# Two dispatch scatters in flight at most, in a two-layer MoE kernel on one core

## What is computed

```python
    x = x + _L0_ffn_ref(_L0_cond_ref(x, itok_B_0_15, L0_cond_weights, L0_cond_b), ...)
    x = x + _L1_ffn_ref(_L1_cond_ref(x, itok_B_0_8, L1_cond_W1, ...), ...)
```

## Time and profile before

| | us |
|---|---|
| median of 3 timed runs | 514.65 (514.14 to 516.04) |
| span of the profiled execution | 571.1 |
| PE busy in it | 463.1 (81%) |
| DVE / ACT / POOL busy | 261.9 / 255.9 / 238.0 |
| on the chain that ended last: PE | 63% |
| on the chain that ended last: another core or an unknown queue | 10% |

### The profile page before, as it was taken

The page is one execution under the profiler, slowest core; times in us unless marked ns, Lnnn a source line. Parts: engine busy times, 40 slices in busy tenths (PEclk is TensorE's granted clock), DMA queues, the critical chain, the costliest instruction groups (busy, mean ns, idle before and its releaser), DMA issues.

```text
span 571.1 us, 10130 instructions
## 1 busy us (share of the span) xinstructions
PE 463.1 (81%) x3132; PEld 392.7 (69%) x3133; DVE 261.9 (46%) x831; ACT 255.9 (45%) x596; POOL 238.0 (42%) x255
## 2 busy tenths in 40 slices
PE   6897698978888889999846765489999999999910
PEld 3785564566676766787744655178999999999900
DVE  1144267845555554347447912053433333233475
ACT  2453453235555543556314241034455555555653
POOL 2023535214554555003272777600155555556550
PEclk8997879999999999999787796579999999999975
DMA  9999921102222107400010111110223434313569
GB/s 242 365 340 368 367 66 37 39 23 67 74 71 63 47 11 235 143 2 20 19 51 15 48 48 55 42 47 1 61 76 96 134 107 113 105 50 88 165 182 282
DMA packets 70930, 62.33 MB, mean 109 GB/s; under 512 B 9676, under 2 KB 57439, under 8 KB 70898
## 3 DMA queue, kind: packets, MB, share of 16 engines
q1 hardware_dynamic: 63202, 48.32, 28.5%
q0 software_dynamic: 7168, 12.56, 6.7%
q10 hardware_dynamic: 528, 1.05, 0.6%
HBM read 32.44 MB, written 31.69 MB: 112 GB/s over the span
## 4 chain that ended last, share of the span: by engine, by line
PE 63%; another core or an unknown queue 10%; DVE 9%; DMA 7%; issue 6%; ACT 2%; POOL 1%; SPq 0%; DVEq 0%; POOLq 0%; ACTq 0%
PE PS L1645 11%; PE PS L1304 8%; PE PS L1361 6%; PE PS L1603 5%; PE PS L1441 3%; PE PS L1635 3%; PE PS L1565 3%; PE PS L1633 3%; PE PS L1634 3%; PE PS L1393 2%; PE PS L1402 2%; DMA back1b<-grp_y,grp_i 2%; PE PS L1426 2%; PE PS L1428 1%
## 5 line engine op out<-in xcount | busy, mean ns | idle before, releaser
L623 POOL DMA_INDIRECT back<-grp_y,grp_i x70 | 69.8, 997 | 93.9 <-DVE grp_y L1236 71.0
L605 POOL DMA_INDIRECT rows<-disp,slot x64 | 63.6, 994 | 76.1 <-DVE slot L1072 56.0
L1645 PE MATMUL PS<-w2r,act 128*128 128x128 f32 x640 | 78.1, 275 | 0.5 <-ACT act L789 0.5
L1645 PEld LDWEIGHTS PS<-w2r,act 128*128 128x128 f32 x640 | 74.8, 192 | 0.9 <-DVE grp_y L1236 0.7
L582 POOL DMA_INDIRECT back<-act,blk_i x48 | 46.9, 977 | 60.8 <-DVE act L1015 41.1
L789 ACT ACTIVATE act<-PS,b1r 128x256 f32<-128x256 f32 x160 | 63.7, 477 | 16.5 <-PE PS L1635 14.2
L571 POOL DMA_INDIRECT rows<-disp,slot x32 | 32.6, 1018 | 67.4 <-issue 53.8
L1236 DVE TENSOR_TENSOR grp_y<-PS,b2r 128x256 f32<-128x256 f32 x40 | 17.0, 424 | 89.6 <-PE PS L1645 69.5
L1603 PE MATMUL PS<-sw,act 128*128 128x128 f32 x256 | 37.5, 313 | 14.1 <-issue 11.8
L1633 PE MATMUL PS<-xh,w1h 128*128 128x256 f32 x160 | 48.3, 302 | 0.0
L740 ACT ACTIVATE act<-PS,sb 128x512 f32<-128x512 f32 x32 | 21.4, 688 | 59.6 <-remote 32.9
(11 more groups left out here) (256 smaller groups left out, 1009.9 us busy)
## 6 DMA issues: line engine op xcount, KB each, us to landing
rows<-zrow SPq DMA_DIRECT2D x32, 260.0 KB, 5.0
grp_x<-rows SPq DMA_DIRECT2D x40, 130.0 KB
w_raw<-in_f_gate_up SPq DMA_DIRECT2D x8, 512.0 KB, 10.1
back<-zrow SPq DMA_DIRECT2D x8, 512.0 KB
back<-back SPq DMA_DIRECT2D x16, 256.0 KB, 5.0
blk_x<-rows SPq DMA_DIRECT2D x48, 65.0 KB
acc<-in_x SPq DMA_DIRECT2D x8, 256.0 KB, 5.8
y0g<-back SPq DMA_DIRECT2D x8, 256.0 KB, 3.2
```

Of the source, the lines that this page charges most:

```text
L605: gp.indirect_dma_start(rows1, bass.IndirectOffsetOnAxis(ap=slot[:, k, t:t + 1], axis=0), disp[:, t, :], None, bounds_check=E1 * CAP - 1, ...
L623: gp.indirect_dma_start(back, bass.IndirectOffsetOnAxis(ap=grp_i[v % NX][:, u:u + 1], axis=0), grp_y[k][:, u, :], None, bounds_check=last, ...
L1645: last = mm(PS[5 + k][:, u * P:(u + 1) * P], act[k][:, c, u * P:(u + 1) * P], w2r[e][:, c, :], start=c == 0, stop=c == C1 - 1)
```

## The change

Each dispatch scatter but the first two of each layer waits until the scatter two before it has landed. For that the semaphores are shared out otherwise: by the parity of the tile, not by group (layer 0) or by half (layer 1). The wait for the whole half ahead of the rewrite of the codes goes away, since the new waits imply it.

```diff
+                if t >= 2:
+                    pool.wait_ge(sc0[t % 2], 16 * (t // 2))
                 gp.indirect_dma_start(rows0, bass.IndirectOffsetOnAxis(ap=slot[:, 0, t:t + 1], axis=0),
                                       disp[:, t, :], None, bounds_check=NBLKP * P - 1,
-                                      oob_is_err=False).then_inc(sc0[t // G % 2], 16)
+                                      oob_is_err=False).then_inc(sc0[t % 2], 16)
...
+                    n = k * NT + t
+                    if n >= 2:
+                        pool.wait_ge(sc1[(n - 2) // NT][t % 2], 16 * ((n - 2) % NT // 2 + 1))
                     gp.indirect_dma_start(rows1, bass.IndirectOffsetOnAxis(ap=slot[:, k, t:t + 1], axis=0),
                                           disp[:, t, :], None, bounds_check=E1 * CAP - 1,
-                                          oob_is_err=False).then_inc(sc1[k][t // HT], 16)
+                                          oob_is_err=False).then_inc(sc1[k][t % 2], 16)
                     if (k, t) in ((0, NT - 8), (1, HT - 8)):
                         h = k
-                        pool.wait_ge(sc1[0][h], 16 * HT)
```

## The result

The changed kernel takes 538.61 us (median of 4 runs, 538.06 to 540.67) and the kernel before 514.76 (4 runs beside it, 514.14 to 516.04): a ratio of 1.0458 with a 95% interval of 1.0412 to 1.0503, slower by 23.9 us. The forecast was 522.2 in a range of 513 to 529, so the sign was right, the size was a third of the real one, and the range did not hold it. The profiled execution took 538.72 us and has a span of 536.6. Its own time fits the span and the median; the span of the first profile (571.1) did not.

What follows compares the result with a forecast made beforehand. Without stalls, layer 1's dispatch scatters were taken to bound the expert phase. Layer 1 adds 9 us, 1.5 lost to slack, layer 0 adds 0: 514.65 + 7.5 = 522.2 us, range 513 to 529.

Steps and rivals of the forecast that it cites:

- The stalls are of one execution: Mostly beside layer 1's scatters: nearly all of the 56.5 us between profiled span and timed median belongs to the profiled execution.
- The dispatch scatters, not PE, open the expert phase: Layer 1 without stalls: sorted rows arrive at 360.8 us, PE is ready at 351, so scatters are last by some 10.
- With 1.5 us of the 9 lost to slack: Layer 1's added 9 us at the end of the scatter chain, counted as 7.5 in timed runs.
- Release to start 0.80: POOL in layer 1: a scatter that waits starts 0.80 us after its release, with 0.30 to 0.87 as bounds.
- Landing 2.1: Layer 1: a scatter lands 2.1 us after its start, taken between 1.81 and 2.35.
- +0.16 for each: Layer 1's pace: (2.1 + 0.8) / 2 = 1.45 us a scatter against 1.29 before, so 0.16 us more for each.
- Cost 0: Layer 0: its slower scatters stay covered before PE's first block and cost nothing.
- Round three starts at 79.3 anyway: Layer 0: round two's end moves from 68 to 79 us without delaying the third round, which starts at 79.3.
- the cover 13.2 us: Layer 0: from SP's block loads at 106.35 to PE's first block read at 119.56, 13.2 us less the load.
- Hidden: Rival 1, chance 0.21: pace untouched or PE last by more than 6 us; time 514.65, within 513 to 517.
- Faster: Rival 2, chance 0.12: stalls are real queueing partly in timed runs, limiting scatters removes some; -10 to 0, about 507 us.
- Much slower: Rival 3, chance 0.05: layer 0 landings under load take 10 us, PE waits some 3 us at its first block; 525 us.

Runs made afterwards that it cites:

- the codes on ACT: Layer 1's rewrite of the expert codes moved from POOL to ACT, scatters not limited, against the kernel before: 515.85 us, ratio 0.9983.

## Why the prediction was wrong in size

**The stalls are of one execution: right.** None of the ten later profiles has a wait for an unknown queue of that kind, and the kernel before has a span of 515.1. What caused them stays open.

**"The dispatch scatters, not PE, open the expert phase": right**, rebuilt with 10 us, measured 5.35. The places of the rebuild were late: SP's load stood at 357.6 and comes at 343.36, since the first scatter of layer 1 already starts at 250.40 and not at 265.26. So 14.9 us were lost ahead of the stretch that I cleaned, where I had allowed 3.5. "With 1.5 us of the 9 lost to slack" was wrong: there was none, and I had hedged towards the side that my own rebuild spoke against.

**"Release to start 0.80": right** (0.8). **"Landing 2.1"** was too short: 2.29 at the usual least, up to 2.84 when late. The Trainium skill (DMA: Bandwidth & Descriptors, "Anatomy of one DMA") gives an estimate of 2.15 us from its figures, which the trace supports to 0.14 us where a landing is not late. It holds for the landing alone. With the landing alone as the price of a place, half of 2.29 is below 1.29 and nothing would be lost; the 0.8 us of release make the difference.

**The first failing step is "+0.16 for each".** A pair takes 3.10 us (349.54 to 352.64), a landing of 2.3 and a release of 0.8, so 1.55 for a scatter and not 1.45: +0.26 against 1.29. Late landings add about 0.06 more. In all the mean is 1.67 against 1.346 in the kernel before (both with the gaps around the rewrites), 0.32 for each of 55 intervals, 17.8 us where I had 9 for the 56. That this equals my own upper end, "+0.32", is in part chance: it came from a landing of 2.35 and a release of 0.87, without late landings. Of the difference of two nearly equal numbers, 1.45 and 1.29, an error of 0.1 us is more than half. The range should have held it; I cut it there.

**The second is "Cost 0" in layer 0**, measured 5.9 us with the limit in that layer alone. The ends of rounds one and two were forecast well (62 and 79; their last scatters start at 58.5 to 63 and at 81). Two things behind them were not. "Round three starts at 79.3 anyway" was read from the profile with the stalls; without them and without the limit its first scatter, the 17th, starts at 69 to 75 us, so the 8 to 14 us that it then comes later, at 83, are not hidden. And "round four ends 1.2 us later": SP's load, at 94.7 to 101 us where the limit doesn't reach it, starts at about 111, not "about 107.6". Nor was "the cover 13.2 us": the rows are there at 112.8, and PE would have been ready at 106.7 to 109.1, which leaves waits of 4.1 to 6.2 us. I had cleaned layer 1 of the stalls and left layer 0 as it stood, though I wrote myself of some 3.5 us of the same kind there. How much cover there is varies: of six later profiles in which PE doesn't wait for the block, it reads it between 106.4 and 109.1 us in four, at 112.91 (the kernel before) and 114.85 (the codes on ACT) in two. The granted clock goes with it. It is the third number from the end of a row, as a share of full speed; the rows are 40 to 60 us of the kernel before, profiled again, and of the limit in layer 1 alone:

```profile
40.00:60.00 20.00, 15.72 (x123) 13.73 (x123) 9.50 (x33) 10.82 (x21) 9.77 (x10) 0.91 1.05 367
...
40.00:60.00 20.00, 17.95 (x157) 16.45 (x156) 9.84 (x34) 13.96 (x28) 12.46 (x13) 1.00 1.05 364
```

It is 0.91 in both late profiles and 1.00 in the other four, and the 24 matmuls of one row (lines 1361, 1362, 1368), which take 2.81 us with the limit in layer 1 alone, take 4.14 and 4.47 in the late ones. That is some 1.5 of the 4 to 8 us; what makes the rest is open.

**The sum**: PE's longer wait in layer 1 is 17.7 us and its wait in layer 0 is 6.2, together 23.9, and 23.9 us is what the timed runs lost. That they agree to the tenth is luck, for the limits one at a time add up to 21.7 us. The two profiles of before and after differ by 21.5 us, and in them PE reads the first block of layer 0 at the same time (112.91 and 112.84), since PE was late by itself in the former. The wait there costs its full length only in executions in which PE is ready at 107 to 109 us; that such executions are the usual ones is argued from the 5.9 us of the limit in layer 0 alone.

**The rivals.** *Hidden* fell: the release is 0.8 and there is no slack. *Faster* fell: the time rose, and the kernel before, profiled again, shows no unknown wait that could be saved. *Much slower* named the right place, PE's first block in layer 0, but not the reason: it asked for landings of 10 us, and 5 to 7 were enough.

## What to carry to other kernels

A limit on transfers in flight costs (landing + release) / n - issue for each, as soon as that is above zero; read landing and release from a row in which the engine does wait. The number in flight that cost nothing that shows was (landing + release) / issue rounded up: 3.1 / 1.29 = 2.4, so three. Where a chain of 56 such steps opens the next phase, the cost is multiplied by 56, so a tenth of a microsecond in the term is worth more thought than the rest. A profile whose span is far from the timed runs has to be cleaned everywhere or taken again, since cover and slack read from it are as wrong as its total.

## What the runs showed of the hardware

A wait of POOL on a semaphore that has long been reached costs it nothing: 0.30 us between scatters with it and without it. Where it does have to wait, about 0.8 us pass from the landing to the start. A scatter beside zero fills that move some 360 GB/s lands after 5.1 to 7.0 us, against 2.29 us beside nothing; with two in flight the first eight there take 24.9 us (38.67 to 63.54), one each 3.1 us. And one profiled execution in eleven had 56 us of stalls that no timed run shows.
